# Second feed-forward weight split later, its x2T in halves, and stack slots fetched in two steps

## The reference

```python
x1 = _ln(x) * (scale1 + 1.0) + shift1
qkv = (x1 @ mat_qkv_w.T + qkv_bias).reshape(B, L, 3, H, hd)
q = _l2norm(q) * sm
k = _l2norm(k)
scores = jnp.einsum('bhqd,bhkd->bhqk', q, k)
probs = jax.nn.softmax(scores, axis=-1)
o = jnp.einsum('bhqk,bhkd->bhqd', probs, v)
attn_out = o @ proj_w.T + proj_b
x = x + attn_out * gamma1
x2 = _ln(x) * (scale2 + 1.0) + shift2
h = jax.nn.gelu(x2 @ fc1_w.T + fc1_b, approximate=False)
ffn_out = h @ fc2_w.T + fc2_b
x = x + ffn_out * gamma2
```

## Time and profile before

| | us |
|---|---|
| runs: lowest, median, highest of 3 | 834.9, 837.64, 839.46 |
| the profiled execution | 836.95 |
| its span (first to last instruction) | 835.2 |
| its mean granted TensorE clock | 0.979 |

### The profile page before, as it was taken

How to read it: one execution, slowest core, us unless ns; L and a number is a source line. 1 busy time by engine, 2 the same in 40 slices (tenths; PEclk the granted TensorE clock), 3 DMA queues, 4 the chain that set the end, 5 groups by cost and what they waited for, 6 DMA issues and landing times.

```text
span 835.2 us, 15488 instructions
## 1 busy us (share of the span) xinstructions
PE 766.2 (92%) x4964; PEld 561.5 (67%) x4964; DVE 491.3 (59%) x1010; ACT 477.6 (57%) x765; POOL 380.8 (46%) x638
## 2 busy tenths in 40 slices
PE   4989999999997589999999999999868999999997
PEld 3878778787875345666666666666545888888885
DVE  1378888888887555666666665565453443444433
ACT  1334444444444357777777777777745655555553
POOL 0157575757575655555555555554560212222110
PEclk9989999999999789999999999999979999999999
DMA  8701212131300666566666666666710000000001
GB/s 246 245 23 48 94 48 93 47 93 47 93 13 13 115 114 114 115 111 113 113 115 109 107 112 115 114 110 112 118 20 1 0 26 26 26 26 14 26 24 40
DMA packets 68604, 65.59 MB, mean 79 GB/s; under 512 B 10832, under 2 KB 67792, under 8 KB 68560
## 3 DMA queue, kind: packets, MB, share of 16 engines
q1 hardware_dynamic: 67232, 64.87, 36.6%
q10 hardware_dynamic: 1328, 0.16, 0.1%
HBM read 48.09 MB, written 16.78 MB: 78 GB/s over the span
## 4 chain that ended last, share of the span: by engine, by line
PE 64%; ACT 11%; DVE 10%; issue 7%; POOL 2%; DMA 1%; SPq 1%; ACTq 0%; DVEq 0%; POOLq 0%
PE ps L1567 10%; PE ps L1581 10%; PE ps L1293 6%; PE ps L1457 5%; PE ps L1443 5%; ACT probsT L820 4%; PE ps L1495 3%; PE ps L1395 3%; PE ps L1334 3%; PE ps L1269 2%; PE ps L1284 2%; PE ps L1323 2%; PE ps L1476 2%; ACT w_ada L849 2%; ACT weightT L757 1%
## 5 line engine op out<-in xcount | busy, mean ns | idle before, releaser
L820 ACT ACTIVATE probsT<-ps 128x1024 f32<-128x1024 f32 x128 | 130.9, 1023 | 48.7 <-PE ps L1443 48.7
L1191 DVE TENSOR_TENSOR hidden_low<-hidden,hidden_high 128x512 fp32r<-128x512 f32 x64 | 46.6, 728 | 107.2 <-ACT hidden_high L931 59.2
L1097 DVE TENSOR_REDUCE neg_max<-ps 128x4 bf16<-128x344 f32 x128 | 64.2, 512 | 56.7 <-PE ps L1410 55.9
L1443 PE MATMUL ps<-q_stack,k_stack 97*128 97x256 bf16 x512 | 79.5, 278 | 10.4 <-ACT probsT L820 6.2
L1443 PEld LDWEIGHTS ps<-q_stack,k_stack 97*128 97x128 bf16 x512 | 43.1, 98 | 67.0 <-ACT probsT L820 30.4
L928 ACT ACTIVATE hidden<-ps,b_fc 128x512 f32<-128x512 f32 x64 | 44.1, 689 | 69.6 <-PE ps L1567 69.6
L1457 PE MATMUL ps<-probsT,v_ones 128*32 128x256 f32 x1024 | 68.5, 385 | 9.2 <-ACT probsT L820 9.1
L608 POOL TENSOR_TENSOR scores<-scores,row_max 128x640 f32<-128x640 f32 x32 | 40.8, 1276 | 76.6 <-DVE row_max L966 76.6
L1387 PE MATMUL ps<-w_qkv,x1T 128*128 128x512 f32 x128 | 64.8, 631 | 2.8 <-DVE rest L1104 2.8
L1293 PE MATMUL ps<-x_res,w_q 128*128 (+1 forms) x256 | 62.9, 390 | 0.0
L1293 PEld LDWEIGHTS ps<-x_res,w_q 128*128 128x128 f32 x256 | 46.8, 192 | 10.8 <-issue 5.5
(11 more groups left out here) (173 smaller groups left out, 1893.2 us busy)
## 6 DMA issues: line engine op xcount, KB each, us to landing
parts_dram<-w_ada SPq DMA_DIRECT2D x96, 128.0 KB
q_stack<-parts_dram SPq DMA_DIRECT2D x96, 128.0 KB, 4.3
adj<-in_adj SPq DMA_DIRECT2D x16, 440.0 KB, 4.2
k_stack<-parts_dram SPq DMA_DIRECT2D x16, 384.0 KB, 7.7
xT<-in_xT SPq DMA_DIRECT2D x16, 256.0 KB, 3.0
x_in<-in_x SPq DMA_DIRECT2D x16, 256.0 KB, 2.7
k_stack<-parts_dram SPq DMA_DIRECT2D x16, 256.0 KB, 8.6
out_x<-result SPq DMA_DIRECT2D x16, 256.0 KB, 2.1
```

Source lines behind the costliest of these rows:

```text
L820: nc.scalar.activation(probsT[:, s % 4, :], ps[:, COLS:COLS + 2, :].rearrange("p a n -> p (a n)"), ACT.Exp).then_inc(exp_made, 1)
L1097: nc.vector.tensor_reduce(places[:, :, k], ps[:, ROW_BANKS[n % 2], 0:4 * KP].rearrange("p (a g) -> p a g", a=4), AX_X, ALU.max, negate=Tru ...
L1191: nc.vector.tensor_tensor(hidden_parts[1][:, s % H_SLOTS, :], hidden[:, s % RAW, :], hidden_parts[0][:, s % H_SLOTS, :], ALU.subtract).the ...
L1443: mm = nc.tensor.matmul(ps[:, COLS + j, kt * N:(kt + 1) * N], k_stack[:, par, place, kt * P:(kt + 1) * P], q_stack[:, par, place, :], star ...
```

## The change

- GpSimd: the first weight's split stands ahead of `ffn_root(0)`. The second weight's split also waits for x2_low, that is for both of VectorE's `first_x2`; its wait on stores counts only those of the high and middle parts.
- ScalarE: `ffn_scale(0)` is called one channel block at a time, behind the exponentials of slots 0 and 1.
- PE: `first(0)` and `first(1)` move from slots 2 and 4 to slots 4 and 6. Behind the turns `first(3)` moves ahead of `second(0)`.
- SyncE: the high and middle slots (five of q_stack's six, and five of k_stack's six in three DMAs) are fetched as soon as the high and middle parts are stored, ahead of the store of the low parts; the two slots with low parts are fetched behind it. There are ten fetches instead of nine, and the low stores count on a semaphore of their own, low_out.

The diff without the lists of semaphore names:

```diff
-    FIRST_AT = (2, 4)
+    FIRST_AT = (4, 6)
...
         def put_part(n, par, part, made):
             for w in range(2):
                 sp.wait_ge(made, 2 * n + w + 1)
-                sp.dma_start(parts_dram[w, :, part], parts[:, par, w, part]).then_inc(parts_out, 16)
-
-        def get_stacks(n, par):
-            sp.wait_ge(parts_out, 6 * 16 * (n + 1))
+                sp.dma_start(parts_dram[w, :, part], parts[:, par, w, part]).then_inc(low_out if part == 2 else parts_out, 16)
...
+        def get_high_and_mid(n, par):
+            sp.wait_ge(parts_out, 4 * 16 * (n + 1))
             ge(sp, st_mm, n * 8 - 8)
...
-            for slot, part in enumerate(Q_PARTS):
-                sp.dma_start(rows(q_stack, slot, 1), whole(0, part, 1)).then_inc(stack_in, 16)
-            for slot, n in ((0, 3), (3, 2), (5, 1)):
-                sp.dma_start(rows(k_stack, slot, n), whole(1, 0, n)).then_inc(stack_in, 16)
+            for slot in range(NSLOT - 1):
+                sp.dma_start(rows(q_stack, par, slot, 1), whole(0, Q_PARTS[slot], 1)).then_inc(stack_in, 16)
+            for slot, m in ((0, 2), (3, 2), (5, 1)):
+                sp.dma_start(rows(k_stack, par, slot, m), whole(1, 0, m)).then_inc(stack_in, 16)
+
+        def get_low(n, par):
+            sp.wait_ge(low_out, 2 * 16 * (n + 1))
+            sp.dma_start(rows(q_stack, par, NSLOT - 1, 1), whole(0, 2, 1)).then_inc(stack_in, 16)
+            sp.dma_start(rows(k_stack, par, 2, 1), whole(1, 2, 1)).then_inc(stack_in, 16)
...
             if b is not None:
+                get_high_and_mid(b, 1 - par)
                 put_part(b, 1 - par, 2, low_made)
-                get_stacks(b, 1 - par)
+                get_low(b, 1 - par)
                 max_row(b, 1 - par, 0)
             if f is not None:
-                ge(sp, stack_in, f * (9 * 16))
+                ge(sp, stack_in, f * (10 * 16))
...
                 pool.wait_ge(g["late_weights"], g["LATE"])
+                split(w_fc1, w1_high, w1_low, w1_split)
                 ffn_root(0)
-                split(w_fc1, w1_high, w1_low, w1_split)
             if isinstance(c, int) and c == B - 1:
-                pool.wait_ge(parts_out, 6 * 16 * B)
+                pool.wait_ge(parts_out, 4 * 16 * B)
                 pool.wait_ge(s_mm, GROUPS * B)
+                pool.wait_ge(x2_low, C2)
                 split(w_fc2, w2_high, w2_low, w2_split)
...
-            ge(act, parts_out, 6 * 16 * (f - 1))
+            ge(act, parts_out, 4 * 16 * (f - 1))
...
                     act.wait_ge(s_mm, GROUPS * B)
-                    ffn_scale(0)
                 if c is not None and s < 8:
                     probabilities(c, s)
+                if isinstance(c, int) and c == B - 1 and s < C2:
+                    ffn_scale(0, (s,))
...
-                pe.wait_ge(stack_in, 9 * 16 * (c + 1))
+                pe.wait_ge(stack_in, 10 * 16 * (c + 1))
...
-            if s < STEPS:
+            if s < STEPS and s != LEAD + 1:
                 first(s)
-            if s == 2:
+            if s == LEAD:
                 output_tokens(B - 1, None, COLS)
+                first(LEAD + 1)
```

More of the change, by code:

```diff
@@ L484, in stages @@
     (stats_made, mv_made, eps_made, rstd_made, xhat_made, xt_mm, x1_out, qk_mm, qk_out, v_mm, v_out, sq_made, ss_made,
-     root_step, qkn_made, qkt_mm, high_made, rest_made, mid_made, low_made, parts_out, stack_in, s_mm, max_made, m_mm, m_out,
+     root_step, qkn_made, qkt_mm, high_made, rest_made, mid_made, low_made, parts_out, low_out, stack_in, s_mm, max_made, m_mm, m_out,
      m_low_in, m_high_in, st_mm, exp_made, pv_mm, os_out, otok_mm, den_made, otok_made, ot_mm, ot_out, proj_mm, proj_out,
@@ L489, in stages @@
         "v_out", "sq_made", "ss_made", "root_step", "qkn_made", "qkt_mm", "high_made", "rest_made", "mid_made", "low_made",
-        "parts_out", "stack_in", "s_mm", "max_made_a", "m_mm", "m_out", "m_low_in", "m_high_in", "st_mm", "exp_made_a",
+        "parts_out", "low_out", "stack_in", "s_mm", "max_made_a", "m_mm", "m_out", "m_low_in", "m_high_in", "st_mm", "exp_made_a",
         "pv_mm_a", "os_out", "otok_mm", "den_made", "otok_made", "ot_mm", "ot_out", "proj_mm", "proj_out", "res_mm",
@@ L554, in put_part, with rows, whole @@
                 sp.wait_ge(made, 2 * n + w + 1)
-                sp.dma_start(parts_dram[w, :, part], parts[:, par, w, part]).then_inc(parts_out, 16)
-        def get_stacks(n, par):
-            sp.wait_ge(parts_out, 6 * 16 * (n + 1))
-            ge(sp, st_mm, n * 8 - 8)
[L561 to L565, removed]
-            for slot, part in enumerate(Q_PARTS):
-                sp.dma_start(rows(q_stack, slot, 1), whole(0, part, 1)).then_inc(stack_in, 16)
-            for slot, n in ((0, 3), (3, 2), (5, 1)):
-                sp.dma_start(rows(k_stack, slot, n), whole(1, 0, n)).then_inc(stack_in, 16)
+                sp.dma_start(parts_dram[w, :, part], parts[:, par, w, part]).then_inc(low_out if part == 2 else parts_out, 16)
+        def rows(stack, par, at, n):
+            return stack[at * SLOT:(at + n) * SLOT, par].rearrange("p (h c) n -> p h (c n)", c=C2)
+        def whole(w, part, n):
+            return parts_dram[w, :, part:part + n].rearrange("h a d x -> (a d) h x")
+        def get_high_and_mid(n, par):
+            sp.wait_ge(parts_out, 4 * 16 * (n + 1))
+            ge(sp, st_mm, n * 8 - 8)
+            for slot in range(NSLOT - 1):
[6 more added lines that the diff above has]
+            sp.dma_start(rows(k_stack, par, 2, 1), whole(1, 2, 1)).then_inc(stack_in, 16)
         def turn(f, b, c, d, par):
@@ L885, in turn, with ffn_scale @@
                 take_sums(c, 1)
-        def ffn_scale(n):
+        def ffn_scale(n, channels=range(C2)):
             act.wait_ge(xt_mm_f, n + 1)
             ge(act, x2_low, C2 * n)
-            for k in range(C2):
+            for k in channels:
                 for h in range(2):
```

## The result

Over 12 runs beside 12 of the kernel before, on the same chips, the median is 835.37 us (833.32 to 836.31) against 837.48 us (834.9 to 841.38). The ratio is 0.9963, with a 95% interval of 0.9949 to 0.9977, so some 3.1 us less, 0.37%; the two medians alone lie 2.1 us apart. The forecast was 833.9 us, 3.7 us less than the median known then, and a difference within 0.5% was held the likeliest outcome. The profiled execution took 833.7 us, with a span of 831.9 us, 3.3 us shorter than that of before.

What follows compares the result with a forecast made beforehand. PE, busy 92%, was taken as the bound, held up at the seam by slow x_hat_f, ScalarE's order and the clock. Gains of 0.5 + 2.3 + 0.9 = 3.7 us gave 833.9 us from the 837.64 median; range 829.5 to 839.

Steps and rivals of the forecast that it cites:

- x_hat_f, 2.3 us: VectorE at the seam: with GpSimd quiet, x_hat_f takes 1.38 instead of 3.68 us, 2.3 us on the path.
- First split for nothing: GpSimd: the first weight's split fits the 7.60 us hole, puts the root off by less than 0.1 us, costs nothing.
- second one covered: GpSimd: the second weight's split ends near 623, covered by over 10 us before second(0).
- Halves, and the clock: Last attention turn: x2T in halves gives 3.6 us at full clock, but the clock still falls, leaving 0.9 us.
- The schedule from the first col_scores: Last turn, from col_scores 0: exponential at 0.64 us, second, third and fourth col_scores at 1.72, 3.55 and 5.38 us.
- slow exchange with ScalarE: Last attention turn: one slower exchange between PE and ScalarE at low clock loses some 0.4 us.
- Stacks: SyncE's loop: stacks land about 1 us earlier, turns stay 21.12 us, only the 0.48 us wait at 589.53 goes.
- S: Issue of the store of the high parts in a SyncE turn, 545.99 us in the profile before.
- the rival's late landing: SyncE's loop: low store waits for all fetches, 3.8 us, landing at S + 22.5; late stacks, 844.1 us, chance 0.13.
- first(3): PE, feed-forward: first(3) ahead of second(0) only moves the idle in front of output_channels; gain 0, bounds 0 and 0.9 us.

Runs made afterwards that it cites:

- e1: Kernel before with only GpSimd's two edits: first weight's split ahead of the root, second behind x2_low; ratio 0.9965.
- e6: Changed kernel, but the second weight's split waits for the stores of the low parts instead of x2_low; ratio 0.9994.
- e7: Changed kernel plus six matmuls of no use behind each of the last sample's first three col_scores; ratio 0.9915.
- e8: Changed kernel plus unused matmuls: six behind each of the last sample's first three col_scores, five behind each of the first two a turn earlier; ratio 0.9905.
- e2: Kernel before with only SyncE's new order of stores and fetches; ratio 1.0005.
- e4: Kernel before with GpSimd's two split edits and x2T in halves, without SyncE's order and the move of first(3); ratio 0.9961.
- e5: Changed kernel with first(3) back behind second(0); ratio 0.9955.
- e3: Kernel before with only x2T in halves behind the exponentials and first(0), first(1) in slots 4 and 6; ratio 1.0003.
- e11: Kernel before with unused matmuls: 22 ahead of the first x_hat_f's transposes, 16 and 6 behind the last sample's first two col_scores; ratio 0.9973.

## Why the prediction was right, point by point

- **x_hat_f, 2.3 us.** Right: 1.37 us instead of 3.68, and e1 and e6 show that GpSimd's split beside it is the cause, from both sides. The Trainium skill ("SBUF — State Buffer", section "Who interferes with whom") says that a VectorE copy or tensor_scalar in its two-port mode and a GpSimd operation shut each other out for a whole instruction. The trace agrees: the four took 1.11, 0.69, 1.42 and 0.69 us instead of 0.41, and each of them ended 0.15 us behind the end of a GpSimd subtraction (1.27 us) or cast (0.68 us). VectorE's neg_max, which reads PSUM, took 0.52 us beside the first split as without it.
- **First split for nothing, second one covered.** Right: the root at 601.48 started 6.1 us ahead of its user, x_hat_f at 607.62, and the second split ended near 623.5, over 11 us before second(0) at 635.38.
- **Halves, and the clock.** Right in kind. The schedule from the first col_scores (0.64, 1.72, 3.55, 5.38 us) came out at 0.69, 1.77, 3.60 and 5.42. The clock fell as forecast, at 615.7, though no idle of PE was longer than 1.22 us. The rule of the Trainium skill ("TensorE: Matmul & The Clock Gate", section "Why this matters for your kernels") that was weighed there, that it takes a long unbroken gap to bring the clock down, didn't hold here: the measurement decides. The term was mis-sized: 3.41 us of full work at the low level instead of 4.5, and no slow exchange with ScalarE, so the part is 19.9 us long, not 20.5: 1.5 us gained, not 0.9. At full clock the part is 18.25 us (e7), where the sum said 17.8.
- **Stacks.** Right in kind: landing at S + 21.0 against S + 20.6, turns unchanged, the wait of 0.48 us gone. The rule of the Trainium skill ("DMA: Bandwidth & Descriptors", section "Queues, rings and completion order") that a queue's descriptors are taken in ring order holds in this trace: the low store, issued at 553.97, moves from 559.5. Yet it cost little, and the near hit hides misses that cancel. From S to the first fetch it took 5.6 us, not 4.6; the eight fetches had landed 10.7 us later (10.6 in the sum); the low store held the queue for only 0.9 us more, where I had taken the middle of nothing and 3.8 us; and the low fetches took 3.7 us, near the middle of 2.1 and 4.9. So the rival's late landing, which put 3.8 us on the store, did not come although its rule holds.
- **first(3).** Right: 0.
- **What was not in the sum:** the fall of the clock in the turn before the last. It makes the stretch ahead of the last sample's first col_scores 28.8 us in the changed kernel against 27.2 us in e8, about 1.6 us. Without it the sum of the parts is 2.3 + 1.5 + 0.5 = 4.3 us; with it 2.7, and the seam became 52.5 - 49.8 = 2.7 us shorter. So the forecast of 3.7 us came as near as it did partly by luck: the halves gave 0.6 us more than the sum had, and this fall took 1.6 us. What the sum had wrong is the reading that this turn keeps its clock, because it did in rows 2 (587.35 to 592.77, 2.72 busy of 5.42 us). In the ten profiles without fillers in that turn and with the loop's normal pace it fell in six (changed, e2, e4, e5, e6, e7). The four without it have the old order of SyncE (before, e1, e3, e11), but e4 has the old order and the fall. The kernel before need not be free of it either: 49 of 70 runs of it beside the experiments have a mean granted clock below the 0.979 of its profile, 40 of them 0.977, the value of the profiles of e2 and e6, which have the fall. A mean does not tell where the clock fell, but the profile of before may well be better off in this turn than most of its runs, and the seam's 2.7 us then too small. What decides is open.

## What to carry to other kernels

Where VectorE and GpSimd both work in SBUF, put the work that nobody waits for (here a weight split of 7.7 us) into the stretch where its neighbour idles or reads PSUM: putting one wait back (e6) cost nearly all of the gain. Count what a hand-over of PE and another engine costs in clock as well as in idle time: a turn that began with PE busy 2.26 of 5.86 us lost 1.6 us to it, and 18 matmuls of no use, in gaps that were idle anyway, bought it back. And for changes near the noise compare the intervals inside the profile that the edit can reach, not only totals.

## What the hardware showed that was not expected

The granted clock fell with PE busy 2.26 of 5.86 us and no gap over 1.22 us, and in another turn with gaps of 0.91 and 0.97 us, where other profiles with the same gaps kept it; small matmuls of 0.14 us each in the gaps, 3.83 busy of 5.46 us, kept it. Removing its falls from the seam (e8 against the changed kernel) made it 3.2 us shorter, no less than the best part of the change (3.0 us, e1). And three DMAs of 128 KB more in a turn of 21.1 us cost 37 us in all, part of which may be the clock's: the DMA share over the loop, 0.65 before and 0.61 in the changed kernel (335 to 580 us), looked like room, but the loop of stores and fetches, each waiting for the other to land, had next to none.
